# Third attention: the second score bank's probabilities are scaled on VectorE instead of GpSimd

## The reference, cut to what matters

```
q = einsum('btd,dnh->btnh', layernorm(x), Wq) + bq        # 16 heads of 64
k = einsum('bsd,dnh->bsnh', ctx, Wk) + bk ;  v = the same with Wv, bv
scores = einsum('bsnh,btnh->bnts', k, q) * (1.0 / math.sqrt(float(H)))
adder = (1.0 - attention_mask[:, None, :, :]) * -10000.0
probs = softmax(scores + adder, axis=-1)
x = x + tanh(g_xattn[2]) * (einsum(probs, v) @ Wo + bo)
```

## Time and profile before

| | us |
|---|---|
| median of 3 runs | 1598.7 (1589.78 to 1600.38) |
| the profiled execution: its time | 1599.66 |
| the profiled execution: its span | 1597.9 |
| busy in the span: PE, PEld | 1393.7 (87%), 1155.8 (72%) |
| busy in the span: DVE, ACT, POOL | 850.3 (53%), 767.9 (48%), 424.3 (27%) |

### The profile page before, as it was taken

One profiled execution on the slowest core, in us unless ns is written; L12 is line 12 of the kernel. 1 busy time (PEld: TensorE's weight loads), 2 busy tenths in 40 slices (PEclk: granted clock), 3 DMA queues, 4 the chain that ended last, 5 costly groups with the idle time before them and its releaser, 6 DMA issues. The chain is left out here.

```text
span 1597.9 us, 32065 instructions
## 1 busy us (share of the span) xinstructions
PE 1393.7 (87%) x10658; PEld 1155.8 (72%) x10658; DVE 850.3 (53%) x2171; ACT 767.9 (48%) x1905; POOL 424.3 (27%) x578
## 2 busy tenths in 40 slices
PE   8999878889999999987999999999999998401588
PEld 5888645677799997766888878789999996400355
DVE  4888665766422223005666653832222274688887
ACT  3666453420344435544677673345555522430277
POOL 1000000012122210002333331256666644431141
PEclk9999999899799999998999997889999999755799
DMA  3000020673211126436344432012222343421001
GB/s 108 21 20 15 5 93 1 210 271 64 64 34 39 35 80 208 165 152 215 111 129 143 143 82 93 1 57 94 92 92 93 87 172 128 112 19 10 0 14 40
DMA packets 114518, 140.17 MB, mean 88 GB/s; under 512 B 37072, under 2 KB 93152, under 8 KB 114272
## 3 DMA queue, kind: packets, MB, share of 16 engines
q1 hardware_dynamic: 91872, 85.86, 17.3%
q0 software_dynamic: 11136, 28.93, 6.4%
q10 hardware_dynamic: 11392, 23.86, 4.3%
HBM read 99.96 MB, written 37.49 MB: 86 GB/s over the span
## 5 line engine op out<-in xcount | busy, mean ns | idle before, releaser
L3673 PEld LDWEIGHTS L2f_bank<-L2f_xT,L2f_w_tile 128*128 128x128 f32 x1264 | 154.0, 192 | 7.5 <-ACT L2f_xT L3741 3.5
L3673 PE MATMUL L2f_bank<-L2f_xT,L2f_w_tile 128*128 128x128 f32 x1264 | 154.7, 276 | 3.1 <-ACT L2f_xT L3741 3.1
L3797 DVE TENSOR_TENSOR L2f_hT<-L2f_gate_h,L2f_bank 128x256 f32<-128x256 f32 x79 | 33.3, 421 | 149.1 <-ACT L2f_gate_h L3748 149.1
L906 POOL TENSOR_TENSOR L2x_probs<-L2x_probs,L2x_inv_sum 128x512 f32<-128x512 f32 x64 | 67.8, 1068 | 159.1 <-DVE L2x_inv_sum L1130 159.1
L1047 ACT ACTIVATE L2x_probs<-L2x_shifted,L2x_top 128x128 f32<-128x128 f32 x256 | 99.0, 393 | 14.1 <-DVE L2x_top L1122 14.1
L3596 POOL DMA_INDIRECT L2f_y_rows<-L2f_xn,L2f_put_row x79 | 78.0, 988 | 55.4 <-DVE L2f_xn L3813 51.8
L3735 ACT COPY L2f_w_tile<-L2f_w_up 128x1024 f32 x79 | 82.7, 1047 | 17.7 <-issue 17.7
L3588 POOL DMA_INDIRECT L2f_rows<-L2f_x_rows,L2f_take_row x79 | 76.9, 974 | 45.0 <-DVE L2f_take_row L3561 21.3
L3673 PEld LDWEIGHTS L1f_bank<-L1f_xT,L1f_w_tile 128*128 128x128 f32 x736 | 85.6, 192 | 1.1
L3673 PE MATMUL L1f_bank<-L1f_xT,L1f_w_tile 128*128 128x128 f32 x736 | 85.9, 275 | 0.0
L3690 PE MATMUL L1f_bank<-L1f_w_down,L1f_hT 128*128 x368 | 83.1, 379 | 0.0
(11 more groups left out here) (677 smaller groups left out, 3335.0 us busy)
## 6 DMA issues: line engine op xcount, KB each, us to landing
L1f_w_up<-in_L_ffn_w SPq DMA_DIRECT2D x16, 512.0 KB, 8.6
L1f_w_down<-in_L_ffn_w SPq DMA_DIRECT2D x16, 512.0 KB, 9.3
L2x_k_ahead<-L1f_w_tile ACTq DMA_DIRECT2D x16, 512.0 KB, 2.9
L2x_v_ahead<-L1f_w_tile ACTq DMA_DIRECT2D x16, 512.0 KB, 2.6
L2x_kT<-L2x_k_ahead SPq DMA_DIRECT2D x16, 512.0 KB, 4.6
L2x_v<-L2x_v_ahead SPq DMA_DIRECT2D x16, 512.0 KB, 3.4
L2f_got<-L2f_y_rows SPq DMA_DIRECT2D x16, 512.0 KB, 4.3
L2f_w_up<-in_L_ffn_gate_w SPq DMA_DIRECT2D x16, 256.0 KB, 3.7
```

Source lines behind the costliest of these rows:

```text
L906: nc.gpsimd.tensor_tensor(probs[c][:, :, :], probs[c][:, :, :], inv_sum[:, c, :][:, :, None].to_broadcast([P, 4, P]), ALU.mult).then_inc(s ...
L3673: x = nc.tensor.matmul(products(j, m), w_tile[j][:, at:at + P], xT[j][:, k * P:(k + 1) * P], start=(k == 0), stop=(k == KT - 1))
L3797: nc.vector.tensor_tensor(hT[j][:, 0:F], gate_h[j][:, 0:F], bank[2 + j][:, F:2 * F], ALU.mult).then_inc(q["h"], 1)
```

## The change: what it does

GpSimd keeps the scaling of bank 0. The scaling of bank 1 goes to VectorE, as the last instruction of `invert`, behind both reciprocals of the half batch, with a wait for the second of them. The semaphore that both banks shared becomes two, `scaled0` and `scaled1`, and TensorE waits for the one of the bank that it transposes. The reciprocal of bank 1 no longer waits for the previous scaling of that bank, which now lies on its own engine.

```
@@ on_gpsimd
             def scale_rows(b, r):
-                for c in range(2):
-                    n = b * 4 + (2 * r + c)
-
-                    pool.wait_ge(s["inv"], n + 1)
-                    nc.gpsimd.tensor_tensor(probs[c][:, :, :], probs[c][:, :, :],
-                                            inv_sum[:, c, :][:, :, None].to_broadcast([P, 4, P]), ALU.mult
-                                            ).then_inc(s["scaled"], 1)
+                pool.wait_ge(s["inv"], b * 4 + (2 * r + 1))
+                nc.gpsimd.tensor_tensor(probs[0][:, :, :], probs[0][:, :, :],
+                                        inv_sum[:, 0, :][:, :, None].to_broadcast([P, 4, P]), ALU.mult
+                                        ).then_inc(s["scaled0"], 1)
@@ on_tensor, transposed(b, r)
-                    pe.wait_ge(s["scaled"], n + 1)
+                    pe.wait_ge(s[f"scaled{c}"], b * 2 + (r + 1))
@@ on_vector, invert(b, r)
                     dve.wait_ge(s["exped"], n + 1)
-                    after(dve, s["scaled"], n - 1)
+                    if c == 0:
+                        after(dve, s["scaled0"], b * 2 + r)
                     nc.vector.reciprocal(inv_sum[:, c, :], total[:, c, :]).then_inc(s["inv"], 1)
+
+                dve.wait_ge(s["inv"], b * 4 + (2 * r + 2))
+                nc.vector.tensor_tensor(probs[1][:, :, :], probs[1][:, :, :],
+                                        inv_sum[:, 1, :][:, :, None].to_broadcast([P, 4, P]), ALU.mult
+                                        ).then_inc(s["scaled1"], 1)
```

More of the change, by code:

```diff
@@ L830, in wide_attention @@
             "w_q", "w_o", "biases", "k_in0", "k_in1", "v_in0", "v_in1", "mask_in0", "mask_in1", "mask_add", "xn",
-            "filled", "evicted_act", "evicted_dve", "scores", "shifted", "topped", "exped", "inv", "scaled",
+            "filled", "evicted_act", "evicted_dve", "scores", "shifted", "topped", "exped", "inv", "scaled0", "scaled1",
             "pT", "pT_out", "pv", "headsT", "projected", "updated", "passed",
```

## The result

The changed kernel takes 1587.78 us in the median of 19 runs (1582.09 to 1591.32), beside 1597.66 us for 19 runs of the kernel before on the same chip. The ratio is 0.9942 with a 95% interval of 0.9927 to 0.9957. Of 1597.66 us that is 9.3 us less, 6.9 to 11.7 by the interval; the two medians differ by 9.9. Forecast were 9.3 us less. VectorE's busy time is 870.0 us and GpSimd's 388.6 us.

What follows compares the result with a forecast made beforehand. TensorE's queue was taken as the bound, only its gaps winnable. 15 batches at 0.57 us plus 0.4 and 0.3 at the ends give 9.3 us off 1598.7: 1589.4 us, range 1580.5 to 1599.5.

Steps and rivals of the forecast that it cites:

- What bounds the stage: TensorE's queue sets the pace; its wait for scaled probabilities in r = 1, 0.76 us a batch, is the most to win.
- The hold: VectorE's scaling of bank 1 is held until GpSimd's running instruction ends, and then needs 0.54 us.
- Who starts first: In r = 1 GpSimd starts 0.2 us ahead; were VectorE ahead, only 0.7 us would be gained, chance 0.12.
- The rest of the batch: Mask 0.22 us, GpSimd's scaling 1.04, `shift` of r = 0 near 819.1, bank 1 of r = 0 0.7 to spare.
- third rival: VectorE's chain becomes the bound at r = 1's bank 1, from 0.8 us added a batch; 1608 us, chance 0.05.
- The sum: Over the block, 15 batches at 0.57 us give 8.6 us; with 0.4 and 0.3 at the ends, 9.3 us.
- The ends: Bank 1's waits shrink: 0.4 off 0.68 us in the first half batch, 0.3 of 0.88 in the last.

Runs made afterwards that it cites:

- VectorE first: The changed kernel, but GpSimd waits for the second reciprocal of a half batch instead of the first: 1601.68 us, 1.0027 of the kernel before.
- change, again: The changed kernel itself, measured again as reference beside the kernel without bank 1's scaling: 1589.55 us, 0.9949 of the kernel before.
- the same, bias earlier: The changed kernel with both banks scaled on VectorE and the first batch's bias made between r = 0's two reciprocals: 1585.67 us, ratio 0.9931.
- one more on VectorE: The changed kernel plus one unread 128 x 512 reduction on VectorE behind the scaling of r = 1: 1589.65 us, 0.9956 of the kernel before.
- three more: The changed kernel plus three unread 128 x 512 reductions on VectorE behind the scaling of r = 1: 1608.87 us, 1.0084 of the kernel before.
- bank 1 unscaled: The changed kernel without bank 1's scaling; its transposes wait for the reciprocal instead: 1582.93 us, 0.9905 of the kernel before.
- bank 1 unscaled, again: The changed kernel without bank 1's scaling, measured a second time beside the change: 1585.6 us, 0.9918 of the kernel before.

## Why the prediction was right, and where not

**What bounds the stage: right.** The gap of r = 1 was nearly all there was to win. Moving the scaling in r = 1 alone gives the 13.58 us, in r = 0 alone 14.17.

**The hold: right, within 0.01 us.** Worked out was that VectorE is held until GpSimd ends and then needs 0.54 us; measured 0.55, in r = 1 behind the scaling and in r = 0 behind the bias. The estimate came from a row with half the columns. That what remains after the release is less than a free scaling (0.691 us on VectorE, 1.04 on GpSimd) is seen in both directions: GpSimd, when second, ended 821.57 + 1.54 - (821.52 + 0.69) = 0.90 us after VectorE, not 1.04. The rule in the Trainium skill, "SBUF — State Buffer", section "Who interferes with whom", that issue order and not the kind of operation decides who is blocked, agrees with the pair of kernels: 1.57 and 1.04 us with GpSimd first, 0.69 and 1.545 with VectorE first. What the second pays is somewhat less than a wait for the whole of the first plus its own time.

**Who starts first: right, by less than said.** 0.2 us were worked out for GpSimd's lead in the loop; from 789 us on the batches alternate between 0.02 and 0.33 to 0.41. It decides 0.53 us a batch, as the kernel with VectorE first shows, and with 0.02 it held.

**The rest of the batch: right.** The mask takes 0.215 us in the median instead of 1.06, GpSimd's 1.18 became 1.04, and `shift` of r = 0 starts at 818.55. VectorE's idle time ahead of the second reciprocal of r = 0 is 1.27 us. In r = 0 VectorE has bank 1 ready at 824.42, and TensorE comes to it at 824.66 + 0.43 = 825.09: 0.67 to spare, 0.7 worked out.

**The place of the third rival: wrong.** Its wait was named at r = 1, from 0.8 us on. It comes first at r = 0, whose own slack of 0.7 the prediction had worked out a few lines earlier and not compared with the 0.8. With 1.8 us added, both banks of r = 0 wait. No wait for VectorE's probabilities arises in r = 1 there.

**The sum: its total right by luck, its terms less so.** It counted 15 batches at 0.57 us. From the trace, with the first matmul of each `project` as marks, 13 intervals are whole; these are 13.57 or 13.58 us with the change and 14.02 to 14.18 before, 7.5 us together and not 8.6. The last two intervals, in which parts of a batch are missing, take 19.09 us in the change and its repeat and 19.05 before: nothing is won there. Ahead of the whole ones lie two pieces: `start`, from the first transposes of normalised rows to the second, in which TensorE waits for no scaling yet, and `first`, from there to the first `project`. In us, with the mean granted clock of TensorE in brackets (it is 1.00 in all the whole intervals):

| kernel | `start` | `first` | 13 whole | last two | together |
|---|---|---|---|---|---|
| before | 15.83 (0.83) | 26.59 (0.87) | 183.95 | 19.05 (0.91) | 245.4 |
| change | 17.89 (0.67) | 24.34 (1.00) | 176.49 | 19.09 (0.91) | 237.8 |
| change, again | 15.96 (0.72) | 25.94 (0.87) | 176.47 | 19.09 (0.91) | 237.5 |
| r = 1 only | 15.85 (0.83) | 25.85 (0.87) | 176.50 | 17.40 (1.00) | 235.6 |
| r = 0 only | 15.93 (0.72) | 26.66 (0.87) | 183.85 | 19.09 (0.91) | 245.5 |
| both on VectorE | 14.38 (0.95) | 26.29 (0.94) | 175.85 | 18.29 (0.91) | 234.8 |
| the same, bias earlier | 15.62 (0.82) | 24.26 (1.00) | 175.84 | 19.01 (0.91) | 234.7 |
| VectorE first | 17.74 (0.66) | 27.73 (0.88) | 183.35 | 21.76 (0.84) | 250.6 |
| one more on VectorE | 14.21 (0.87) | 25.91 (0.87) | 177.52 | 19.24 (0.91) | 236.9 |
| three more | 15.80 (0.83) | 26.61 (0.87) | 192.76 | 20.35 (0.92) | 255.5 |
| bank 1 unscaled | 15.74 (0.83) | 22.69 (1.00) | 177.72 | 16.61 (1.00) | 232.8 |
| bank 1 unscaled, again | 14.54 (0.87) | 25.23 (0.86) | 177.72 | 16.61 (1.00) | 234.1 |

The 13 whole intervals and the last two repeat to 0.02 us where a kernel was profiled twice. `start` varies by 3.7 us without a scaling in it: in the change it is long at a clock of 0.67 and behind a wait of 3.06 us for the query weights, in its repeat that wait is 1.67. `first` is to be compared at like clocks: 26.59 before and 25.94 in the repeat of the change, both at 0.87.

The block is 7.6 us shorter in the profile of the change and 8.0 in its repeat, not 9.3; the interval of the ratio holds both. The time outside the block differs by up to 13 us between these profiles (1346.7 to 1359.7), so a single span's 9.4 says little, and that the forecast total was met so closely is luck.

**The ends: the waits as forecast, the gain not.** In the first half batch 0.4 us were forecast of a wait of 0.68: 0.27 of it is left in the repeat, and nothing in the first profile, where TensorE had been slow just before (a granted clock of 0.61 from 732.8 to 738.9 us). In the last half batch 0.3 us were forecast: bank 1's wait went from 0.88 to 0.58, but the last two intervals are no shorter. Behind that wait TensorE's clock falls, before as with the change, and `project` takes longer. The change:

```profile
952.49 1.06 PE L968 MATMUL L2x_bank<-ident,L2x_probs 128*128 128x128 f32 x4 [0.58 <-DVE L2x_probs L1131]
953.34 4.94 PE L990 MATMUL L2x_bank<-L2x_wo,L2x_headsT 128*128 128x256 f32 x16
```

And VectorE in r = 1 only:

```profile
948.32 0.66 PE L972 MATMUL L2x_bank<-ident,L2x_probs 128*128 128x128 f32 x4 [0.57 <-DVE L2x_probs L1139]
948.82 3.62 PE L994 MATMUL L2x_bank<-L2x_wo,L2x_headsT 128*128 128x256 f32 x16
```

In the change the granted clock is 0.50 (the 1.2 GHz level) from 953.0 to 956.0 us; in the other kernel it is 1.00 (2.4 GHz) from 940 to 957, behind waits of 0.77, 1.73 and 0.57 us, where the change has 0.77, 1.72 and 0.58. The 1.7 us between their last two intervals are therefore the clock's, and why it fell in the one and not in the other is not shown.

Not foreseen: `make_bias` stands on VectorE behind the new scaling, and TensorE's wait for it is 2.01 us, though only 0.51 in the repeat. TensorE's timeline of the first two batches, change:

```profile
740.34 1.04 PE L968 MATMUL L2x_bank<-ident,L2x_probs 128*128 128x128 f32 x8
749.68 1.21 PE L968 MATMUL L2x_bank<-ident,L2x_probs 128*128 128x128 f32 x8 [0.64 <-POOL L2x_probs L903]
756.50 0.44 PE L935 MATMUL L2x_bank<-ident,L2x_xn 128*128 128x128 f32 x2 [2.01 <-DVE L2x_bo L1151]
```

The repeat:

```profile
738.70 0.66 PE L968 MATMUL L2x_bank<-ident,L2x_probs 128*128 128x128 f32 x4 [0.27 <-DVE L2x_probs L1131]
747.65 1.96 PE L968 MATMUL L2x_bank<-ident,L2x_probs 128*128 128x128 f32 x8 [0.64 <-POOL L2x_probs L903]
755.57 0.44 PE L935 MATMUL L2x_bank<-ident,L2x_xn 128*128 128x128 f32 x2 [0.51 <-DVE L2x_bo L1151]
```

Here the eight transposes at 748 to 750 us took 1.21 us in the one and 1.96 in the other, where the granted clock was 1.00 from 749.6 to 752.6 us and 0.51 from 747.6 to 751.0 (the 2.4 and the 1.2 GHz level). That fits a chain through VectorE that has more time while TensorE is slow, so that less of it shows as a wait.

So what the scaling on VectorE costs at the ends is read at like clocks. Both the change and the unscaled kernel run `first` at 1.00: 24.34 against 22.69 us, 1.65 less without the scaling, and most of it is the wait for the bias, 2.01 against this one:

```profile
754.85 0.44 PE L935 MATMUL L2x_bank<-ident,L2x_xn 128*128 128x128 f32 x2 [0.73 <-DVE L2x_bo L1149]
```

In the repeats, at 0.87 and 0.86, it is 25.94 against 25.23, 0.7 less. The last two intervals, at 1.00, are 17.40 with r = 1 only and 16.61 unscaled, 0.8 less. Against this the 13 whole ones are 1.2 us longer unscaled. By these profiles the scaling costs 0.3 to 1.2 us in all; the rest of the 3 to 6 us between those kernels and the change lies in `start`, in the clock at the end and outside the block, and no run ties it to the change: it stays open.

The missed expectation of VectorE first is also one of the ends. Its whole intervals are 14.04 to 14.11 us, as expected, and together 0.6 us shorter than before, but `first` is 1.1 us longer (TensorE's first two sets of transposes of r = 0 and r = 1 wait 0.96 and 1.98 us for GpSimd), and the last two intervals are 2.7 longer, behind a wait of 3.77 us for GpSimd and at a clock of 0.84 where it was 0.91. `start` is 1.9 longer too, but without a scaling in it.

## What to carry to other kernels

Look for the gap in the full engine's stream and move the one instruction that is late there, not the load of the engine that does the most of that kind: here one scaling in a batch gave all, and the other one moved gave nothing. Where VectorE and GpSimd are to scale tiles of SBUF at the same time, look in the trace whether they take turns, as they did here; a split then pays only by the shorter tail of the second, and it hangs on who starts first, so it is worth trying all of it on the faster engine (the same time here, and no order to keep). Sum a gain over the intervals that are whole in the trace, and read the first and last batches by themselves and at like granted clocks: there TensorE waits for other chains, and the clock moved more than the change did.

## What the runs showed of the hardware

- A scaling of 128 x 512 with both inputs in SBUF takes 0.691 us on VectorE alone and 1.04 on GpSimd alone. Held by GpSimd's from nearly the same start it takes 1.57, and GpSimd's held by VectorE's 1.545. The two together need 1.59 us, two on VectorE alone 1.50.
- A lead of 0.05 us between the records' starts was enough for VectorE to go first, and one of 0.02 us for GpSimd.
- Held work costs the second engine less than its whole duration after the release: 0.55 of 0.69 us on VectorE, 0.90 of 1.04 on GpSimd.
